# Products of state and C for two successive states in one GpSimd instruction, in a selective-scan recurrence

## The chip, the cores and the metric

The kernel runs on one core of one Trainium2 chip. The metric is the device time of one execution in microseconds, given as the median of several runs. A core has five engines with instruction queues of their own (TensorE for matmuls, VectorE, ScalarE, GpSimd, and SyncE, which here issues most DMAs). They meet through semaphores.

## The reference

Three layers follow each other on an input of shape (4, 64, 32, 32): a Mamba layer applied twice (to x and to x with its channels shuffled), causal attention, and a routed chain of feed-forward and attention steps. The change lies in the Mamba layer. Cut to its recurrence:

```
dt = softplus(x_dbl[..., :dt_rank] @ W_dt.T + b_dt)
A = -exp(A_log)
def step(h, inp):
    dt_t, B_t, C_t, u_t = inp
    dA = exp(dt_t[..., None] * A)
    h = dA * h + (dt_t * u_t)[..., None] * B_t[:, None, :]
    return h, einsum('bdn,bn->bd', h, C_t)
y = ys + u * D_skip
out = y * silu(z) @ W_out.T
```

There are 8 sequences (4 images, 2 kinds), each of length L = 1024, with 128 inner channels d and 16 states n. All is fp32.

## The kernel before, in words

The 128 inner channels lie on the partitions and the 1024 positions along the free dimension. The work is cut into 128 units: unit u is state n = u mod 16 of sequence q = u div 16. For each unit:

- the decay exp(dt * A_n), 128x1024, is made on ScalarE (L1155);
- the driving term dtu * B_n is made in one of two ways. For nine of the sixteen states TensorE broadcasts B_n into the PSUM bank pair pb (L690) and VectorE multiplies it by dtu (L1429). For the seven states in POOLED = (1, 4, 6, 8, 10, 12, 14) a DMA broadcasts B_n from DRAM into bb, and GpSimd multiplies (pool_drive, L1733, the tile dbu); ScalarE then writes the decay of that unit to pb;
- VectorE runs the scan h = decay * h + drive along the 1024 positions (L1434) into one of NHH = 4 buffers hh;
- GpSimd multiplies hh by C_n, which a DMA has broadcast into one of NCC = 4 buffers cc (pool_hc, L1722), into one of NHC = 3 buffers hc;
- TensorE adds hc to the PSUM accumulator py by matmuls with an identity (pe_sum, L702), LAG = 3 units behind.

After unit 15 VectorE multiplies py by the gate (dve_y, L1443, two halves), ahead of unit LAG of the next sequence. Between the units each engine does, at fixed states, pieces of the preparation of the next sequence: the input projection (pe_x, L633 and L634, at n = 0), the B and C rows (n = 3 to 6), and dt as a softplus (n = 7 to 12), with two VectorE steps called lost (L1405, after units 9 and 10) and two called dtu (L1415, after units 11 and 12). In sequences 2, 4 and 6 TensorE also does the output matmuls of a finished image (L721 at n = 13, L729 at n = 14). In sequence 7 the preparation of the attention takes the place of the next sequence: four VectorE steps (t1) after unit 6 and two (zq) after unit 12.

Every engine's order is written out by hand in loops over u. What ties them:

- GpSimd: the driving term of unit u + 2 comes ahead of the product of unit u; the product waits for the scan of u (scan_done), for C (c_in), and for the sum of unit u - NHC (hc_used);
- VectorE: the scan of unit u waits for its driving term, its decay, and the product of unit u - NHH (hc_done);
- TensorE, in iteration u: the B matmuls of unit u + 1 (they wait for the scan of u - 1), then the sum of unit u - LAG (it waits for hc_done), then the pieces of the next sequence;
- SyncE: C of unit u is requested when the product of u - NCC is done; B for pooled unit u + 3 follows it in the queue.

After the last unit TensorE's queue holds the first Q and K matmuls (pe_qk, L824 and L825), the early output matmuls (L721), and the last sums mixed with them.

Of the kernel before, what the change touches and what calls it, by code (L numbers as in the profile page):

```python
# [12 lines left out]
ALU = mybir.AluOpType  # L13
# [3 lines left out]
B, C, L = 4, 64, 1024  # L17
DI, NS, DR = 128, 16, 4
# [14 lines left out]
def atleast(eng, sem, value):  # L33

    if not isinstance(value, int) or value > 0:
        eng.wait_ge(sem, value)
# [332 lines left out]
def build_all(nc, w, inp, scr, out):  # L369

    ctx = ExitStack()
    with ctx:
        def sb(name, shape, dt=FP32):
            return ctx.enter_context(nc.sbuf_tensor(name, shape, dt))
# [6 lines left out]

        POOLED = (1, 4, 6, 8, 10, 12, 14)
        NP = len(POOLED)
        NHH, NHC, NCC, NDA, NDB, LAG = 4, 3, 4, 3, 2, 3
        LAST, UNITS, SKIP_AT, AHEAD = NSEQ - 1, NS * NSEQ, 8, 1

        u2_all = sb("u2_all", [DI, 2 * L])
# [11 lines left out]
        da = [sb(f"da_{i}", [DI, L]) for i in range(NDA)]  # L399
        hh_all = sb("hh_all", [DI, NHH * L])  # L400
        hh = [hh_all[:, i * L:(i + 1) * L] for i in range(NHH)]
        hc = [sb(f"hc_{i}", [DI, L]) for i in range(NHC)]
        cc = [sb(f"cc_{i}", [DI, L]) for i in range(NCC)]
        bb = [sb(f"bb_{i}", [DI, L]) for i in range(2 if NP else 0)]
        dbu = [sb(f"dbu_{i}", [DI, L]) for i in range(NDB if NP else 0)]
        ex, rl = sb("ex", [DI, L]), sb("rl", [DI, L])
# [5 lines left out]
        b_full, dbu_done, da_done, scan_done = sem("b_full"), sem("dbu_done"), sem("da_done"), sem("scan_done")  # L412
        pooled_done, hc_done, hc_used = sem("pooled_done"), sem("hc_done"), sem("hc_used")
# [22 lines left out]
        def pool_count(u):  # L436
            return NP * (u // NS) + sum(1 for n in POOLED if n < u % NS)

        def own_count(u):
            return u - pool_count(u)  # L440

        def outs_before(q):
            return max(0, (q - 1) // 2)
# [249 lines left out]
        def pe_sum(pe, u):  # L693
            if u < 0:
                return
            q, n = divmod(u, NS)
            pe.wait_ge(hc_done, u + 1)
            for r in range(2):
                if n == 0:
                    atleast(pe, y_free, 2 * (q - 1) + r + 1)  # L700
                for t in range(2):
                    last = nc.tensor.matmul(py[part(t), half(r)], ident[part(r), part(r)], hc[u % NHC][part(r), half(t)],  # L702
                                            start=(n == 0), stop=(n == NS - 1), skip_group_check=True)
                last.then_inc(hc_used, 1)
# [115 lines left out]
        def pe_qk(pe, c):  # L820
            pe.wait_ge(zq_done, c + 1)
            if c < 2:
                pe.wait_ge(scan_done, UNITS - 1 + c)
            nc.tensor.matmul(qk[c][0], w["wq1"][:, :], zq[:, col(c)], start=True, stop=True).then_inc(at.q_full, 1)  # L824
            nc.tensor.matmul(qk[c][1], w["wk1"][:, :], zq[:, col(c)], start=True, stop=True).then_inc(at.k_full, 1)  # L825
# [120 lines left out]
        def _(pe):  # L946
# [35 lines left out]
            for u in range(UNITS):  # L982
# [26 lines left out]
                if q == LAST:  # L1009
                    pe_first_pair(pe, n)  # L1010
            pe_qk(pe, 0)
            pe_first_pair(pe, NS)
            pe_sum(pe, UNITS - 3)
            pe_qk(pe, 1)
# [404 lines left out]
        def dve_unit(dve, u):  # L1419
            q, n = divmod(u, NS)  # L1420
            if n == 0:
                dve.wait_ge(dtu_done, 2 * q + 2)
            if pooled(u):
                dve.wait_ge(pooled_done, pool_count(u) + 1)
                decay, drive = pb[u % 2], dbu[pool_count(u) % NDB]
            else:
                k = own_count(u)
                dve.wait_ge(b_full, k + 1)
                nc.vector.tensor_tensor(pb[u % 2][:, :], pb[u % 2][:, :], dtu[q % 2][:, :], ALU.mult).then_inc(dbu_done, 1)  # L1429
                dve.wait_ge(dbu_done, k + 1)  # L1430
                decay, drive = da[k % NDA], pb[u % 2]
            dve.wait_ge(da_done, u + 1)
            atleast(dve, hc_done, u - NHH + 1)
            nc.vector.tensor_tensor_scan(hh[u % NHH][:, :], decay[:, :], drive[:, :], 0.0,  # L1434
                                         ALU.mult, ALU.add).then_inc(scan_done, 1)

# [275 lines left out]
            run(dve, dve_attend, dve_feed, dve_select)  # L1712


        def pool_hc(pool, u):
            pool.wait_ge(scan_done, u + 1)
            pool.wait_ge(c_in[u % NCC], 16 * (u // NCC + 1))
            if u < 2:
                for v in ((2,), (1, 3))[u]:
                    pool.wait_ge(xs_in[v], 32)  # L1720
            atleast(pool, hc_used, 2 * (u - NHC + 1))
            nc.gpsimd.tensor_tensor(hc[u % NHC][:, :], hh[u % NHH][:, :], cc[u % NCC][:, :], ALU.mult).then_inc(hc_done, 1)  # L1722

        def pool_drive(pool, u):
            if u >= UNITS or not pooled(u):
# [47 lines left out]
        def _(pool):  # L1773
# [55 lines left out]
            affine(1, 1)  # L1829
            for u in range(2):  # L1830
                pool_drive(pool, u)
            for u in range(UNITS):
                pool_drive(pool, u + 2)
                pool_hc(pool, u)
            pool.wait_ge(hc_used, 2 * UNITS)
            for t in wa:
                nc.gpsimd.memset(t, 0.0).then_inc(zeroed, 1)
# [47 lines left out]
        def sp_c(sp, u):  # L1885
            q, n = divmod(u, NS)
            if n == 0:
                sp.wait_ge(scr_in, 16 * (q + 1))
            atleast(sp, hc_done, u - NCC + 1)
            sp.dma_start(cc[u % NCC][:, :], scr[q % 2, NS + n:NS + n + 1, :].broadcast_to((128, L))).then_inc(c_in[u % NCC], 16)  # L1890

        def sp_b(sp, u):
# [132 lines left out]
```

## Time and profile before

| | |
|---|---|
| median of 3 runs | 763.95 us (763.78 to 768.19) |
| span of the profiled execution | 766.2 us |
| from its start to the first unit | 46 us |
| recurrence, 46 to 476 us | 430 us: GpSimd busy 426.75, VectorE 403.52, TensorE 331.65, ScalarE 288.99 |
| the rest, 476 to 766 us | 290 us: TensorE busy 247.62, VectorE 146.05, GpSimd 26.16 |

The profile is of one execution, on the one core. No time other than its span is recorded for the profiled execution, so the 766.2 us stand beside the median of the runs and not beside a time of its own. Busy time is the sum of the durations of an engine's instructions, overlaps counted once. A row of the timeline gives the start and duration in us, the engine, the line, the tiles and shapes and a count of merged instructions; in brackets stands idle time before it and what ended it. Successive instructions of one engine overlap slightly in their recorded durations, so the step from start to start is the better measure where there are several in a row.

### The profile page before, as it was taken

What the parts mean: (1) busy time and instruction counts of PE and PEld (TensorE: products, weight loads), DVE (VectorE), ACT (ScalarE), POOL (GpSimd) and SP (SyncE); (2) the same over time, 40 slices, a digit from 0 to 9 for tenths busy, and PEclk for the clock granted to TensorE, in tenths of its full rate; (3) what the DMA queues carried; (4) which work ended last, traced back from release to release, by engine and by line L of the source; (5) the groups of instructions that cost most, each with busy time, mean ns of one, the idle gap of its engine ahead of it and who ended that gap; (6) DMA issues with size and microseconds to landing.
All of it is one profiled execution on the core that took longest, in us unless ns stands there. A gap on an engine that the chain in (4) does not pass through costs nothing.

```text
span 766.2 us, 10774 instructions
## 1 busy us (share of the span) xinstructions
PE 607.6 (79%) x3563; PEld 257.1 (34%) x3591; DVE 570.3 (74%) x587; ACT 440.7 (58%) x662; POOL 474.0 (62%) x252
## 2 busy tenths in 40 slices
PE   3876686777986777967868879978976969999993
PEld 2321121121221212311212223446663335777741
DVE  3488998998998999999989997445562525666643
ACT  1887767587578677676775752544444224555520
POOL 6369999999999999999999998500002200000002
PEclk9999798898998998997989999989999889999997
DMA  3389677576665676666765761000000000000002
GB/s 96 83 266 297 220 240 234 199 260 232 215 237 216 223 255 216 241 229 204 261 231 201 255 228 58 1 1 2 2 12 3 6 15 1 2 1 2 1 2 60
DMA packets 33187, 105.47 MB, mean 138 GB/s; under 512 B 6997, under 2 KB 7518, under 8 KB 33118
## 3 DMA queue, kind: packets, MB, share of 16 engines
q1 hardware_dynamic: 32022, 103.94, 40.1%
q8 instruction: 34, 0.56, 0.3%
q10 hardware_dynamic: 776, 0.55, 0.3%
q0 software_dynamic: 320, 0.13, 0.1%
q14 instruction: 35, 0.29, 0.1%
HBM read 98.84 MB, written 2.10 MB: 132 GB/s over the span
## 4 chain that ended last, share of the span: by engine, by line
issue 34%; PE 24%; POOL 16%; DVE 15%; ACT 7%; DMA 2%; POOLq 0%; SPq 0%; DVEq 0%; ACTq 0%
POOL dbu L1733 7%; POOL hc L1722 7%; DVE hh_all L1434 7%; PE py L702 6%; DVE pb L1429 3%; PE py L229 2%; PE pb L198 2%; PE pb L690 2%; PE px L252 1%; PE px L729 1%; DMA cc<-scr 1%; POOL yg L1736 1%; DVE yg L1443 1%; ACT pb L1155 1%; DVE dtu_all L1415 1%
## 5 line engine op out<-in xcount | busy, mean ns | idle before, releaser
L1722 POOL TENSOR_TENSOR hc<-hh_all,cc 128x1024 f32<-128x1024 f32 x128 | 299.2, 2367 | 2.8 <-DMA cc<-scr 1.5
L702 PE MATMUL py<-hc,w_cst 64*64 64x512 f32 x1024 | 157.0, 673 | 26.3 <-POOL hc L1722 17.9
L1736 POOL TENSOR_TENSOR yg<-w_xs 128x512 f32<-128x512 f32 x12 | 15.2, 1266 | 247.2 <-DVE w_xs L1560 154.6
L1434 DVE TENSOR_TENSOR_SCAN hh_all<-da,pb 128x1024 f32<-128x1024 f32 x72 | 164.6, 2287 | 2.5
L1434 DVE TENSOR_TENSOR_SCAN hh_all<-pb,dbu 128x1024 f32<-128x1024 f32 x56 | 127.7, 2281 | 17.8 <-POOL dbu L1733 14.4
L1733 POOL TENSOR_TENSOR dbu<-bb,dtu_all 128x1024 f32<-128x1024 f32 x56 | 132.6, 2369 | 0.0
L690 PE MATMUL pb<-bc,w_sel 128*128 128x512 bf16 x118 | 42.2, 424 | 71.3 <-DVE hh_all L1434 67.3
L1155 ACT ACTIVATE pb<-dt_all,w_aneg 128x1024 f32<-128x1024 f32 x56 | 62.6, 1118 | 59.9 <-DVE hh_all L1434 58.2
L1429 DVE TENSOR_TENSOR pb<-pb,dtu_all 128x1024 f32<-128x1024 f32 x72 | 87.5, 1215 | 1.8 <-DVE dtu_all L1415 0.2
L285 DVE TENSOR_REDUCE gate_all<-pb 128x1 f32<-128x1024 f32 (+7 forms) x64 | 60.4, 986 | 32.8 <-PE pb L208 16.8
L1155 ACT ACTIVATE da<-dt_all,w_aneg 128x1024 f32<-128x1024 f32 x72 | 80.5, 1137 | 0.5
L702 PEld LDWEIGHTS py<-hc,w_cst 64*64 64x64 f32 x1024 | 31.0, 140 | 105.1 <-issue 56.9
L198 PE MATMUL pb<-dt_all,u_all 64*128 64x512 f32 (+3 forms) x208 | 51.4, 609 | 2.3 <-DVE w_xs L1506 1.2
L690 PEld LDWEIGHTS pb<-bc,w_sel 128*128 128x128 bf16 x144 | 9.5, 100 | 126.5 <-DVE hh_all L1434 101.7
L229 PE MATMUL py<-w_cst,dbu 128*128 128x128 f32 x208 | 29.4, 281 | 9.2 <-ACT dbu L328 5.3
L328 ACT ACTIVATE bb<-pb,gate_all 128x1024 f32<-128x1024 f32 (+4 forms) x32 | 28.6, 904 | 12.5 <-DVE gate_all L285 12.5
L336 ACT ACTIVATE da<-py 128x512 f32<-128x512 f32 (+2 forms) x28 | 13.7, 533 | 35.8 <-PE py L229 35.7
L336 ACT ACTIVATE cc<-py 128x512 f32<-128x512 f32 (+1 forms) x28 | 14.6, 564 | 33.3 <-PE py L229 33.3
L328 ACT ACTIVATE dbu<-pb,gate_all 128x1024 f32<-128x1024 f32 (+3 forms) x32 | 30.3, 957 | 4.7 <-DVE gate_all L285 4.7
L292 DVE COPY da<-py 128x512 f32<-128x512 f32 (+2 forms) x28 | 16.1, 610 | 20.6 <-PE py L229 20.6
L229 PE MATMUL py<-w_cst,bb 128*128 128x128 f32 x192 | 28.2, 287 | 3.9 <-ACT bb L328 3.9
L292 DVE COPY cc<-py 128x512 f32<-128x512 f32 (+1 forms) x28 | 17.2, 648 | 17.3 <-PE py L229 17.3
(290 smaller groups left out, 952.6 us busy)
## 6 DMA issues: line engine op xcount, KB each, us to landing
cc<-scr SPq DMA_DIRECT2D x128, 512.0 KB, 4.4
bb<-scr SPq DMA_DIRECT2D x56, 512.0 KB, 4.8
w_xs<-hc SPq DMA_DIRECT2D x6, 256.0 KB, 4.6
w_xst<-in_x SPq DMA_DIRECT2D x2, 512.0 KB, 5.3
scr<-bcf SPq DMA_DIRECT2D x8, 128.0 KB, 3.6
w_xs<-dt_all SPq DMA_DIRECT2D x4, 256.0 KB, 6.0
w_xs<-dtu_all SPq DMA_DIRECT2D x4, 256.0 KB, 5.6
out<-yg SPq DMA_DIRECT2D x8, 128.0 KB, 2.7
```

The costliest lines, as they stand in the source:

```text
L198: last = nc.tensor.matmul(self.s[r][:, o + a:o + a + m], self.qt[rows, g * 128:(g + 1) * 128], self.kt[rows, p * L + a:p * L + a + m], sta ...
L229: last = nc.tensor.transpose(self.pt[:, o + j:o + j + 128], self.p[g % 2][r][:, j:j + 128], self.w["cst"][:, IDN:IDN + 128])
L285: self.nc.vector.tensor_reduce(self.nm[:, i:i + 1], self.s[r][:, self.start(g):self.start(g) + 128 * self.blocks(g)], AX.X, ALU.max, negat ...
L292: self.nc.vector.tensor_copy(self.pts[g % 2][0][:, a:a + m], self.pt[:, a:a + m]).then_inc(self.pts_dve, 1)
L328: self.nc.scalar.activation(self.p[g % 2][r][:, 0:n], self.s[r][:, self.start(g):self.start(g) + n], ACT.Exp, bias=self.nm[:, i:i + 1], ac ...
L690: last = nc.tensor.matmul(pb[u % 2][:, half(h)], w["sel"][:, n, :], bc3[q % 2][:, half(h)], start=True, stop=True)
L702: last = nc.tensor.matmul(py[part(t), half(r)], ident[part(r), part(r)], hc[u % NHC][part(r), half(t)], start=(n == 0), stop=(n == NS - 1) ...
L1155: nc.scalar.activation(to[:, :], dt[q % 2][:, :], ACT.Exp, scale=w["aneg"][:, n:n + 1]).then_inc(da_done, 1)
L1429: nc.vector.tensor_tensor(pb[u % 2][:, :], pb[u % 2][:, :], dtu[q % 2][:, :], ALU.mult).then_inc(dbu_done, 1)
L1434: nc.vector.tensor_tensor_scan(hh[u % NHH][:, :], decay[:, :], drive[:, :], 0.0, ALU.mult, ALU.add).then_inc(scan_done, 1)
L1722: nc.gpsimd.tensor_tensor(hc[u % NHC][:, :], hh[u % NHH][:, :], cc[u % NCC][:, :], ALU.mult).then_inc(hc_done, 1)
L1733: nc.gpsimd.tensor_tensor(dbu[k % NDB][:, :], bb[k % 2][:, :], dtu[q % 2][:, :], ALU.mult).then_inc(pooled_done, 1)
```

## The change

The products of two successive units u and u + 1, u even, are made by one GpSimd instruction of 128x2048. The buffers of hc and cc become slices of one tensor each, as those of hh already are, and hc gets a fourth buffer. The first two and the last two units keep single products. hc_done now counts instructions, and hc_count(u) gives the count at which unit u's product is done. On GpSimd both driving terms (units u + 2 and u + 3, where they are pooled) stand ahead of the pair; with the states in POOLED, this moves one of the seven, that of state 1, ahead of the product of state 14. TensorE's sums lag by 4 units, y moves to unit 4, and one more sum stands behind the first Q and K matmuls at the end.

```diff
-        NHH, NHC, NCC, NDA, NDB, LAG = 4, 3, 4, 3, 2, 3
+        NHH, NHC, NCC, NDA, NDB, LAG = 4, 4, 4, 3, 2, 4
...
-        hc = [sb(f"hc_{i}", [DI, L]) for i in range(NHC)]
-        cc = [sb(f"cc_{i}", [DI, L]) for i in range(NCC)]
+        hc_all, cc_all = sb("hc_all", [DI, NHC * L]), sb("cc_all", [DI, NCC * L])
+        hc = [hc_all[:, i * L:(i + 1) * L] for i in range(NHC)]
+        cc = [cc_all[:, i * L:(i + 1) * L] for i in range(NCC)]
...
+        def hc_count(u):
+
+            if u < 2:
+                return u + 1
+            return 2 + u // 2 if u < UNITS - 2 else u + 3 - UNITS // 2
...
         def pe_sum(pe, u):
...
-            pe.wait_ge(hc_done, u + 1)
+            pe.wait_ge(hc_done, hc_count(u))
...
             pe_qk(pe, 0)
+            pe_sum(pe, UNITS - 4)
             pe_first_pair(pe, NS)
             pe_sum(pe, UNITS - 3)
...
         def dve_unit(dve, u):
...
-            atleast(dve, hc_done, u - NHH + 1)
+            atleast(dve, hc_done, hc_count(u - NHH))
...
-        def pool_hc(pool, u):
-            pool.wait_ge(scan_done, u + 1)
-            pool.wait_ge(c_in[u % NCC], 16 * (u // NCC + 1))
+        def pool_hc(pool, u, count):
+
+            pool.wait_ge(scan_done, u + count)
+            for v in range(u, u + count):
+                pool.wait_ge(c_in[v % NCC], 16 * (v // NCC + 1))
...
-            atleast(pool, hc_used, 2 * (u - NHC + 1))
-            nc.gpsimd.tensor_tensor(hc[u % NHC][:, :], hh[u % NHH][:, :], cc[u % NCC][:, :], ALU.mult).then_inc(hc_done, 1)
+            atleast(pool, hc_used, 2 * (u + count - NHC))
+            here = slice(u % NHC * L, (u % NHC + count) * L)
+            nc.gpsimd.tensor_tensor(hc_all[:, here], hh_all[:, here], cc_all[:, here], ALU.mult).then_inc(hc_done, 1)
...
-            for u in range(UNITS):
-                pool_drive(pool, u + 2)
-                pool_hc(pool, u)
+            for u in range(0, UNITS, 2):
+                if u in (0, UNITS - 2):
+                    for v in (u, u + 1):
+                        pool_drive(pool, v + 2)
+                        pool_hc(pool, v, 1)
+                else:
+                    for v in (u, u + 1):
+                        pool_drive(pool, v + 2)
+                    pool_hc(pool, u, 2)
...
         def sp_c(sp, u):
...
-            atleast(sp, hc_done, u - NCC + 1)
+            atleast(sp, hc_done, hc_count(u - NCC))
```

## Rows read from the trace of the kernel before

**Rows 1.** The page: span, and GpSimd's busy tenths in forty slices.

```profile
span 766.2 us, 10774 instructions
...
POOL 6369999999999999999999998500002200000002
```

**Rows 2.** The page's groups: shapes, count, busy, mean ns, idle before and its releaser.

```profile
L1722 POOL TENSOR_TENSOR hc<-hh_all,cc 128x1024 f32<-128x1024 f32 x128 | 299.2, 2367 | 2.8 <-DMA cc<-scr 1.5
...
L1736 POOL TENSOR_TENSOR yg<-w_xs 128x512 f32<-128x512 f32 x12 | 15.2, 1266 | 247.2 <-DVE w_xs L1560 154.6
...
L1434 DVE TENSOR_TENSOR_SCAN hh_all<-pb,dbu 128x1024 f32<-128x1024 f32 x56 | 127.7, 2281 | 17.8 <-POOL dbu L1733 14.4
L1733 POOL TENSOR_TENSOR dbu<-bb,dtu_all 128x1024 f32<-128x1024 f32 x56 | 132.6, 2369 | 0.0
...
L1429 DVE TENSOR_TENSOR pb<-pb,dtu_all 128x1024 f32<-128x1024 f32 x72 | 87.5, 1215 | 1.8 <-DVE dtu_all L1415 0.2
```

**Rows 3.** Timeline of GpSimd: products and sums in a row.

```profile
466.31 9.28 POOL L1722 TENSOR_TENSOR hc<-hh_all,cc 128x1024 f32<-128x1024 f32 x4
...
582.86 2.50 POOL L1736 TENSOR_TENSOR yg<-w_xs 128x512 f32<-128x512 f32 x2 [88.61 <-DVE w_xs L1540]
```

**Rows 4.** Timeline of GpSimd and VectorE, sequence 5, units 8 to 14.

```profile
345.97 4.65 POOL L1722 TENSOR_TENSOR hc<-hh_all,cc 128x1024 f32<-128x1024 f32 x2
...
359.84 6.97 POOL L1722 TENSOR_TENSOR hc<-hh_all,cc 128x1024 f32<-128x1024 f32 x3
...
346.04 2.29 DVE L1434 TENSOR_TENSOR_SCAN hh_all<-pb,dbu 128x1024 f32<-128x1024 f32 x1 [0.62 <-POOL dbu L1733]
...
359.93 2.27 DVE L1434 TENSOR_TENSOR_SCAN hh_all<-pb,dbu 128x1024 f32<-128x1024 f32 x1
```

**Rows 5.** Timeline of GpSimd and VectorE, first units of sequence 0.

```profile
50.62 4.67 POOL L1722 TENSOR_TENSOR hc<-hh_all,cc 128x1024 f32<-128x1024 f32 x2 [1.34 <-DVE hh_all L1434]
...
57.56 4.66 POOL L1722 TENSOR_TENSOR hc<-hh_all,cc 128x1024 f32<-128x1024 f32 x2
...
66.02 2.35 POOL L1722 TENSOR_TENSOR hc<-hh_all,cc 128x1024 f32<-128x1024 f32 x1 [1.50 <-DMA cc<-scr]
...
50.46 2.26 DVE L1434 TENSOR_TENSOR_SCAN hh_all<-pb,dbu 128x1024 f32<-128x1024 f32 x1
...
59.53 2.26 DVE L1434 TENSOR_TENSOR_SCAN hh_all<-pb,dbu 128x1024 f32<-128x1024 f32 x1
```

**Rows 6.** Timeline of VectorE and TensorE, ends of sequences 4 and 5.

```profile
306.72 2.29 DVE L1434 TENSOR_TENSOR_SCAN hh_all<-pb,dbu 128x1024 f32<-128x1024 f32 x1
...
371.38 1.21 DVE L1429 TENSOR_TENSOR pb<-pb,dtu_all 128x1024 f32<-128x1024 f32 x1
...
308.31 3.61 PE L729 MATMUL px<-yg,w_wts 64*64 64x512 f32 x16
...
318.33 1.09 PE L702 MATMUL py<-hc,w_cst 64*64 64x512 f32 x8
```

**Rows 7.** Timeline of VectorE, sequence 7: unit 7, then 8 and 12.

```profile
443.57 1.22 DVE L1429 TENSOR_TENSOR pb<-pb,dtu_all 128x1024 f32<-128x1024 f32 x1
444.83 2.29 DVE L1434 TENSOR_TENSOR_SCAN hh_all<-da,pb 128x1024 f32<-128x1024 f32 x1
447.03 2.27 DVE L1434 TENSOR_TENSOR_SCAN hh_all<-pb,dbu 128x1024 f32<-128x1024 f32 x1
...
459.78 2.26 DVE L1434 TENSOR_TENSOR_SCAN hh_all<-pb,dbu 128x1024 f32<-128x1024 f32 x1
```

**Rows 8.** Timeline of TensorE, end of sequence 7.

```profile
468.70 1.09 PE L702 MATMUL py<-hc,w_cst 64*64 64x512 f32 x8 [0.34 <-POOL hc L1722]
469.72 1.12 PE L824 MATMUL pb<-w_xs,w_wq 128*128 128x512 f32 x2
...
477.93 1.09 PE L702 MATMUL py<-hc,w_cst 64*64 64x512 f32 x8
```

**Rows 9.** Tile cc, 100 to 400 us: C's broadcasts from issue to landing.

```profile
DMA to landing us min/median/max: 3.4/4.3/5.4
```

## The prediction

> **What bounds the kernel now.** I read the page first: busy time per engine in forty slices [rows 1], then the groups by line [rows 2], then the timeline of GpSimd and VectorE over the recurrence. The slices show GpSimd at 9 tenths from the fourth slice to the twenty-fourth. The groups say what fills it: 128 products of 2367 ns and 56 driving terms of 2369 ns, with only 2.8 us of idle time before the products and none before the driving terms. From start to start one such instruction takes less than its duration: four products in a row occupy 9.28 us, so that the step is (9.28 - 2.35) / 3 = 2.31 us [rows 2, 3]. 184 x 2.31 = 425 us is the recurrence. A sequence (16 products, 7 driving terms) takes 23 x 2.31 = 53.2 us.
>
> VectorE is not far behind. From start to start its multiply takes 1.26 us and its scan 2.20 us [rows 7]. A sequence is 9 units with both, 7 with a scan alone, and six half-width steps (lost, dtu, y) that I put at 4 us together from the half of a 1215 ns multiply [rows 2]: 9 x 3.46 + 7 x 2.20 + 4 = 50.5 us. The 14.4 us that it waited for driving terms [rows 2] are those few per cent. So GpSimd sets the pace by about 5%, and any saving on it over 2.7 us per sequence would be cut by VectorE. The question is whether even a smaller saving gets through.
>
> **The saving.** 62 pairs of products become 62 instructions of 128x2048. The trace has no two-input instruction of that size. It has 128x512 and 128x1024: two of 512 in a row occupy 2.50 us at 1266 ns each, a step of 1.24 us [rows 2, 3]. From 1.24 and 2.31 us, each element costs 2.09 ns and each instruction 0.17 us beside its elements, so that a pair takes 2.31 + 2 x 1.07 = 4.46 us instead of 4.63. The bounds are 4.63 (nothing is saved) and 4.3 (twice the fixed part). I take 4.46, since both neighbours are measured and the form is the same. On GpSimd alone that is 62 x 0.17 = 10.3 us.
>
> The Trainium skill (GPSIMD Engine Reference, section Performance versus the Vector engine) gives 4497 ns for a two-input add of 2048 elements per partition. By that figure, as an estimate, the saving would be 0.13 us per pair and the whole sum about 1 us worse.
>
> **What the pairing demands.** Before, the product of unit u started when scan u was done. Now a pair u, u+1 starts only when scan u+1 is done, while the driving term that releases the scan of unit u+2 still stands one instruction ahead, and the scan of u+4 waits for the whole pair. So VectorE must be one unit further on at every even product, and it can't be: it is released by GpSimd itself at units 8 and 10. That handover shows as "0.62 <-POOL dbu" [rows 4]. I follow one sequence from the end of the driving term of unit 10.
>
> Stretch one, to the pair 12, 13. Before: two products, a driving term, two products, a driving term, 6 x 2.31 = 13.87 us, and that is what the rows show, 345.97 to 359.84. Scan 13 was done at 359.93, when scan 14 began [rows 4]. VectorE's chain from the driving term (scans 10 to 13, two multiplies, a "lost" and two "dtu" steps) is thus 13.96 us, in the other sequences 14.0 to 14.2. GpSimd would be ready after 2 x 4.46 + 2 x 2.31 = 13.54 us. The product follows a scan's end by 0.16 us (scan 1 starts at 50.46, which is the end of scan 0, and the first product at 50.62 [rows 5]). So the pair starts at 14.12: it waits 0.58 us.
>
> Stretch two, to the pair 0, 1 of the next sequence: pair, driving term of the next unit 1 (now ahead of the pair 14, 15), pair: 11.23 us. From the 359.93 + 0.16 of the same sequence, GpSimd would be ready at 371.32. Scan 1 was done at 371.38, when the multiply of unit 2 began [rows 6]; with 0.16 us that is a wait of 0.2. But this pair also needs the buffers of units 12 and 13, so the sum of unit 13 on TensorE, which with the lag of four comes behind the B matmuls of unit 2. In sequences without an output that sum ends about where scan 1 does, give or take 0.3. In sequences 2 and 4 TensorE is late: the output matmuls, two sums and the next input projection fill it from 308.31 without a gap, and the sum in that place starts at 318.33 [rows 6], ending near 319.3. GpSimd would be ready at 306.72 + 0.16 + 11.23 = 318.11. The pair starts at 319.43: a wait of 1.3 us, twice.
>
> Stretch three, pairs 0 to 6, four times 6.77 us. VectorE's two scans and the multiply between them are 5.66 us, and 1.18 us more where y (now ahead of unit 4) or a "lost" step falls: about 0.1 to 0.2 us late in all.
>
> A plain sequence is then 14.12 + 11.23 + 0.3 + 27.08 + 0.15 = 52.9 us against 53.2: 0.3 gained of the 1.3 saved. Sequences 2 and 4 are 14.12 + 11.23 + 1.3 + 27.08 = 53.75: 0.5 lost each. From sequence 0 to sequence 6, that is 4 x (-0.3) + 2 x 0.5 = -0.2 us.
>
> **Both ends.** In sequence 0 GpSimd is ahead of VectorE. The pair 2, 3 could start at 57.56, but scan 3 ends at 59.53, where scan 4 starts [rows 5]. The pair starts at 59.69, 2.1 us late. Then a wait for C that is in the rows anyway (1.50 us before 66.02) takes most of it: about 0.6 late after the pair 4, 5 and 0.3 by unit 10.
>
> In sequence 7 VectorE has more to do (four steps of t1 at unit 6, two of zq at unit 12) and runs almost without a gap. Scan 7 of it starts at 444.83 and ends at 447.03 [rows 7], so the pair 6, 7 starts at 447.2, 1.8 us after GpSimd would be ready for it (the pair 4, 5 starts at 438.6). GpSimd then ends the driving term of unit 12 at 447.2 + 2 x 6.77 = 460.7, where VectorE was ready for scan 12 at 459.78: VectorE loses 0.9 us, ends scan 13 at 467.6, and the pair 12, 13 (before: from 466.31) runs from 467.7 to 472.2. TensorE's last chain began with the sum of unit 12 at 468.70 and ran without a gap, by way of the first Q and K matmuls at 469.72, to the last sum at 477.93, 9.23 us [rows 8]. Now Q and K (about 1.9 us, two like the row of Q) go ahead of that sum, and the sum waits for the pair until 472.35; 9.23 - 1.9 = 7.3 us later, at 479.7, comes the last one, 1.7 us late.
>
> What follows is untouched. The memory cover: C for a pair is requested when the pair before the last is done, at least 6.77 us ahead, and landed in 3.4 to 5.4 us [rows 9]; two requests now start together, which I cost at nothing, and at up to 1 us per sequence where it fails. Waits on the y bank and on the bf16 pieces keep their distance, as one y step moves by one unit and its sum with it. Queue order on SyncE is unchanged.
>
> Sum: +0.3 (sequence 0), -0.2 (middle), +1.7 (end) = +1.8, all of it a difference. The profiled execution has a span of 766.2 us and lies 2.2 above the median of the runs; so I put it on the median: 763.95 + 1.8 = 765.7 us. Seen from GpSimd, the 10.3 us saved are spent as 7 x 0.6 before the pair 12, 13, about 4 at the seams, and the rest in the first and last sequence.
>
> **Rivals.** (1) The saving gets through. It needs VectorE to be ahead by a unit; for it speaks that its total is 2.7 us under GpSimd's per sequence, against it the waits of [rows 4]. If only the output seams and half of the other waits occur, some 6 us remain: 758; with a fixed part of 0.3 us, 754. Chance 0.15. (2) A pair of 4.63 us. Then stretch one waits 0.25, output seams 1.0, nothing is gained, and the ends cost the same or 1 us more: 7 x 0.3 + 2 x 1.0 + 3 = +7: 771. It decides from a pair over 4.6 us. Chance 0.10. (3) C is late. Three 512 KB transfers in a burst instead of one by one; the cover is 6.77 us less two SyncE issues, the longest landing 5.4 [rows 9]. From a landing of 6.2 us on, each sequence waits at the pairs 0, 1 and 2, 3: at 1 us each, +7 to +9, so 773. Slower. Chance 0.08. (4) The instruction is not run as one, or VectorE is held up by the longer GpSimd instruction: no row shows a scan lengthened beside a busy GpSimd (2281 ns in the mean of 56 [rows 2]). Chance 0.02, around 775. The forecast, waits eat the saving, 761 to 769, has 0.65.
>
> **Chances.** One per cent, 7.6 us, is about what a measurement of this kernel can tell from no change. Faster by more (under 756.3) takes half of rival 1: 0.08. Slower by more (over 771.6) takes rival 3, 4 and a part of rival 2: 0.12. Within: 0.80. The range from 758 to 771 leaves about 2 in 10 out.
>
> **What would show it.** In the new profile: products of 128x2048 at 4.5 us, 62 of them. GpSimd's busy time near 464 us, with some 11 us of new idle before the products, released by VectorE's scans and, in sequences 2 and 4, by TensorE's sums. VectorE's wait for driving terms smaller, not larger. The last sum near 479.7 us. The prediction is wrong if pairs start without waiting, or if pairs take well under 4.4 us, or if the idle before the products is put down to DMA.

## The result, and the profile after

The changed kernel takes 770.7 us (median of 4 runs, 768.3 to 773.0) beside 764.2 us for the kernel before (4 runs): a ratio of 1.0079, with an interval of 1.0053 to 1.0105. Measured a second time (e1, 6 runs beside 27 of the kernel before) it is 1.0061 [1.0040, 1.0082]. The forecast was 765.7 us, 0.7% less; the time is 0.3 us inside the upper end of the range (758 to 771).

The profiled executions hide this: their spans are 766.2 us before and 766.4 us after. They have to be read by stretches. I cut both at the same instructions: GpSimd's first product, the first memset of the code table behind the recurrence, and the first `yg` of the later stages. The first row is of the kernel before, the second of the one after (start, duration, engine, operation, idle time before it).

```profile
483.61 0.63 POOL L1755 MEMSET w_wts<- 1x646 f32 x1 [3.68 <-PE px L729]
```

```profile
486.76 0.63 POOL L1766 MEMSET w_wts<- 1x646 f32 x1 [3.69 <-PE px L736]
```

From the first product (50.62 and 50.87) to this row are 433.0 us before and 435.9 after: the recurrence has become 2.9 us longer. In e1, and in a new run of the kernel before (e5), the same two stretches are 436.9 and 432.7 us: 4.2 longer. What follows is the same list of instructions in both. The windows of TensorE over the first attention step, the feed-forward step and the second attention step (from:to, length, busy time and count, granted clock, DMA share, GB/s), before and then after:

```profile
483.61:582.86 99.25, 86.84 (x717) 0.95 0.02 3
582.86:603.33 20.47, 13.42 (x52) 0.83 0.02 4
603.33:745.85 142.52, 131.97 (x1085) 0.96 0.02 4
```

```profile
486.76:584.81 98.05, 85.59 (x717) 0.97 0.01 3
584.81:605.02 20.21, 13.46 (x52) 0.83 0.01 4
605.02:746.01 140.99, 130.48 (x1085) 0.98 0.02 4
```

The same 1085 matmuls took 142.5 us at a granted clock of 0.96 and 141.0 us at 0.98. That is 3.0 us over the three stretches, it went against the kernel before in this one execution, and it covers the loss. In the other executions below the second attention step is either 140.4 to 141.0 us or 142.5 to 142.9, whatever the kernel (e5, the kernel before again: 140.7). So I compare the stretch of the recurrence alone ("recurrence" below: first product to that memset), and the medians for the whole.

The groups of the page after that answer to [rows 2], and below them, from the answer that keeps shapes apart, the pairs alone:

```profile
L1442 DVE TENSOR_TENSOR_SCAN hh_all<-pb,dbu 128x1024 f32<-128x1024 f32 x56 | 127.8, 2282 | 19.7 <-POOL dbu L1744 16.0
L1744 POOL TENSOR_TENSOR dbu<-bb,dtu_all 128x1024 f32<-128x1024 f32 x56 | 132.1, 2359 | 0.0
...
L1437 DVE TENSOR_TENSOR pb<-pb,dtu_all 128x1024 f32<-128x1024 f32 x72 | 87.3, 1213 | 1.8 <-DVE dtu_all L1423 0.2
```

```profile
L1733 POOL TENSOR_TENSOR hc_all<-hh_all,cc_all 128x2048 f32<-128x2048 f32 x62 | 280.9, 4531 | 12.1 <-DVE hh_all L1442 6.8 <-PE py L709 4.9 <-issue 0.2
```

GpSimd now has 12.1 us of idle time before the pairs and 1.4 before its four single products (the page gives 13.4 for both), where the products had 2.8: 10.6 us are new (some 11 were forecast). 6.8 us end with a scan of VectorE, 4.9 us with a sum of TensorE. The scans take what they took (2282 ns, 2281 before), and VectorE's wait for driving terms rose from 14.4 to 16.0 us. The pair itself, on GpSimd's timeline in sequence 5, units 10 to 14:

```profile
355.05 4.54 POOL L1733 TENSOR_TENSOR hc_all<-hh_all,cc_all 128x2048 f32<-128x2048 f32 x1 [0.61 <-PE py L709]
359.55 2.35 POOL L1744 TENSOR_TENSOR dbu<-bb,dtu_all 128x1024 f32<-128x1024 f32 x1
361.96 4.51 POOL L1733 TENSOR_TENSOR hc_all<-hh_all,cc_all 128x2048 f32<-128x2048 f32 x1
366.43 2.37 POOL L1744 TENSOR_TENSOR dbu<-bb,dtu_all 128x1024 f32<-128x1024 f32 x1
```

From start to start the pair takes 366.43 - 361.96 = 4.47 us, against 2 x 2.31 = 4.63: 0.155 us saved per pair, 9.6 us for 62. The page gives GpSimd 466.1 us of work.

### The profile page after: what moved, and what is told of

Its sections match the earlier page's. It is cut to its first block, busy times and chain, and to the rows that moved or that the text cites. A ratio compares the mean times of both kernels' runs of the same rounds, so it can differ in the third digit from the quotient of the medians.

```text
span 766.4 us, 10739 instructions
## 1 busy us (share of the span) xinstructions
PE 615.0 (80%) x3591; PEld 260.5 (34%) x3591; DVE 570.2 (74%) x587; ACT 440.0 (57%) x662; POOL 466.1 (61%) x190
## 4 chain that ended last, share of the span: by engine, by line
issue 34%; PE 24%; DVE 19%; POOL 14%; ACT 5%; DMA 1%; POOLq 0%; SPq 0%; DVEq 0%; ACTq 0%
DVE hh_all L1442 9%; POOL hc_all L1733 8%; PE py L709 5%; DVE pb L1437 5%; POOL dbu L1744 4%; PE py L229 2%; PE pb L198 2%; PE px L736 2%; PE px L252 1%; POOL yg L1747 1%; PE pb L697 1%; DVE dtu_all L1423 1%; PE px L674 1%; PE px L675 1%; DMA cc_all<-scr 1%
## 5 line engine op out<-in xcount | busy, mean ns | idle before, releaser
L1733 POOL TENSOR_TENSOR hc_all<-hh_all,cc_all 128x2048 f32<-128x2048 f32 (+1 forms) x66 | 290.1, 4399 | 13.4 <-DVE hh_all L1442 8.1
L709 PE MATMUL py<-hc_all,w_cst 64*64 64x512 f32 x1024 | 154.6, 678 | 1.0 <-POOL hc_all L1733 0.6
L1442 DVE TENSOR_TENSOR_SCAN hh_all<-pb,dbu 128x1024 f32<-128x1024 f32 x56 | 127.8, 2282 | 19.7 <-POOL dbu L1744 16.0
L697 PE MATMUL pb<-bc,w_sel 128*128 128x512 bf16 x144 | 48.7, 423 | 85.8 <-DVE hh_all L1442 83.5
L709 PEld LDWEIGHTS py<-hc_all,w_cst 64*64 64x64 f32 x1024 | 33.3, 143 | 75.7 <-issue 65.1
L198 PE MATMUL pb<-dt_all,u_all 64*128 64x512 f32 (+3 forms) x208 | 49.4, 588 | 2.4 <-DVE w_xs L1514 1.2
L336 ACT ACTIVATE cc_all<-py 128x512 f32<-128x512 f32 (+1 forms) x28 | 14.5, 564 | 31.7 <-PE py L229 31.7
L292 DVE COPY cc_all<-py 128x512 f32<-128x512 f32 (+1 forms) x28 | 17.1, 648 | 17.3 <-PE py L229 17.3
```

The source lines that it names most:

```text
L198: last = nc.tensor.matmul(self.s[r][:, o + a:o + a + m], self.qt[rows, g * 128:(g + 1) * 128], self.kt[rows, p * L + a:p * L + a + m], sta ...
L292: self.nc.vector.tensor_copy(self.pts[g % 2][0][:, a:a + m], self.pt[:, a:a + m]).then_inc(self.pts_dve, 1)
L697: last = nc.tensor.matmul(pb[u % 2][:, half(h)], w["sel"][:, n, :], bc3[q % 2][:, half(h)], start=True, stop=True)
L1733: nc.gpsimd.tensor_tensor(hc_all[:, here], hh_all[:, here], cc_all[:, here], ALU.mult).then_inc(hc_done, 1)
```

## The experiments

"Idle" is GpSimd's idle time before pairs; where a kernel has single products too, theirs is not in it (in e7 the products of units 0, 1, 126 and 127). In e9, e10 and e12 a driving term more stands ahead of the first product, so that the recurrence is measured from a later point than in the other kernels; from the first scan of VectorE to the memset it is 435.4 us before, 435.2 in e9, 432.2 in e10 and 433.5 in e12. The kernel before is 764.4 us beside e1 to e4 (27 runs), 764.0 beside e5 to e8 and 764.7 and 764.9 beside e9 to e11 and e12.

| kernel | recurrence, us | idle, us | median, us | ratio to before, interval |
|---|---|---|---|---|
| before / e5, before again | 433.0 / 432.7 | - | 765.4 (e5) | 1.0009 [0.9993, 1.0026] |
| after / e1, after again | 435.9 / 436.9 | 12.1 / 12.9 | 769.1 (e1) | 1.0061 [1.0040, 1.0082] |
| e2 six product buffers | 433.6 | 9.6 | 767.9 | 1.0043 [1.0023, 1.0063] |
| e3 chosen pairs | 433.6 | 7.8 | 767.1 | 1.0031 [1.0014, 1.0047] |
| e4 chosen pairs, six buffers | 433.1 | 7.5 | 767.1 | 1.0036 [1.0017, 1.0054] |
| e6 no pairs | 432.6 | - | 765.4 | 1.0006 [0.9984, 1.0029] |
| e7 waits of pairs alone | 441.2 | 9.2 | 773.8 | 1.0132 [1.0106, 1.0159] |
| e8 pairs at units 4, 6, 8 | 433.6 | 5.2 | 767.5 | 1.0047 [1.0031, 1.0063] |
| e9 pairs, driving terms earlier | 431.9 | 11.0 | 762.7 | 0.9966 [0.9939, 0.9992] |
| e10 driving terms earlier, no pairs | 428.9 | - | 762.0 | 0.9964 [0.9942, 0.9986] |
| e11 pairs at 4, 6, 8, but not at the ends | 432.3 | 2.7 | 765.9 | 1.0023 [1.0003, 1.0043] |
| e12 driving terms earlier, 42 chosen pairs | 430.2 | 2.4 | 761.2 | 0.9948 [0.9930, 0.9965] |

**e1, the same kernel again**, to have a second profile of it beside the runs that follow.

> The changed kernel once more, with a profile from another execution. Theory W (the pairs' waits eat the saving): the recurrence ends 3 us later than before, whichever execution is profiled, and what the median shows beyond 3 us lies in the attention steps after it, where the two executions profiled so far already differ by 3 us; the median falls between 767 and 771. Rival T (the change costs something after the recurrence): the stretch from the end of the recurrence to the end is longer than before's by 3 us in every execution, median 770 to 772.

The recurrence was 436.9 us, the idle time 12.9 us. The three stretches behind it took 259.2 us, and 260.0 in e5: the change costs nothing there. Sequence 1 took 53.7 us here and 52.7 in the first profile, and this difference has a cause that can be read. In its units 7 to 10 stand the matmuls of the time step (L674, L675), which wait for ScalarE. TensorE's timeline there, after and then e1:

```profile
132.29 1.04 PE L697 MATMUL pb<-bc,w_sel 128*128 128x512 bf16 x2 [4.35 <-DVE hh_all L1442]
...
135.53 1.13 PE L674 MATMUL px<-ex,w_cst 128*128 128x512 f32 x2 [0.28 <-ACT px L1131]
136.49 1.02 PE L675 MATMUL px<-rl,w_cst 128*128 128x512 f32 x2
```

```profile
131.78 0.60 PE L697 MATMUL pb<-bc,w_sel 128*128 128x512 bf16 x2 [3.69 <-DVE hh_all L1442]
...
135.60 2.07 PE L674 MATMUL px<-ex,w_cst 128*128 128x512 f32 x2 [1.75 <-ACT px L1131]
137.47 1.91 PE L675 MATMUL px<-rl,w_cst 128*128 128x512 f32 x2
...
139.31 1.23 PE L709 MATMUL py<-hc_all,w_cst 64*64 64x512 f32 x8
...
140.78 4.54 POOL L1733 TENSOR_TENSOR hc_all<-hh_all,cc_all 128x2048 f32<-128x2048 f32 x1 [1.26 <-DVE dtu_all L1423]
```

The same four matmuls take 2.1 us in the one and 4.0 in the other: from 135 to 140 us the granted clock was 0.96 in the first profile and 0.53 in e1, which ran them at the lower of the clock's two levels (1.2 GHz in place of 2.4). The sum behind them ends at 139.31 + 1.23 = 140.54, and the next pair (last row, GpSimd) starts 0.24 us later, after a wait of 1.26 us that it did not have in the first profile. The row names a step of VectorE that ended at about the same time; the same 0.24 us lie between the end of the sum and the pair where the row names TensorE (354.81 and 355.05 in the first profile). Of seven such places the first profile has five in which L674 takes 1.8 to 2.1 us instead of 1.1, e1 all seven; the kernel before had five too (at 188.51, for instance) and no product there waited for TensorE.

**e2, six buffers for the products** (as in all kernels below that mix sizes, a slice is taken per tile by its own number of buffers).

```diff
-        NHH, NHC, NCC, NDA, NDB, LAG = 4, 4, 4, 3, 2, 4
+        NHH, NHC, NCC, NDA, NDB, LAG = 4, 6, 4, 3, 2, 4
```

> The changed kernel with six hc buffers instead of four, so that no pair waits for a sum on TensorE. Theory W: the 4.9 us of GpSimd idle time that TensorE ended (two of 1.4 us at the seams after sequences 2 and 4, and three smaller) go; 1 to 2 us come back as waits for scans; 3 us faster than the changed kernel. A rival (VectorE is the limit and TensorE's waits are hidden anyway): within 1 us of the changed kernel.

```profile
L1738 POOL TENSOR_TENSOR hc_all<-hh_all,cc_all 128x2048 f32<-128x2048 f32 x62 | 280.7, 4531 | 9.6 <-DVE hh_all L1447 9.3 <-DMA cc_all<-scr 0.2
```

Against the 4.9 us of the row after, nothing is left behind TensorE; part of it came back behind VectorE (9.3 against 6.8). The recurrence is 2.3 to 3.4 us shorter than with four buffers: the waits for TensorE's sums cost about 3 us, where I had charged 2 x 1.3. The median moved by only 1.2 us (769.1 to 767.9), and the intervals of the two ratios overlap.

**e3 and e4, pairs only where the plan saw room** (units 2, 4, 6, 8, 10 and 14, without unit 2 of the first and 6 and 14 of the last sequence; e4 with six buffers as well).

```diff
-                if u in (0, UNITS - 2):
+                if not paired(u):
...
+        def paired(u):
+            q, n = divmod(u, NS)
+            return n in (2, 4, 6, 8, 10, 14) and (q, n) not in ((0, 2), (LAST, 6), (LAST, 14))
```

> Pairs only where VectorE is ahead: states 2, 4, 6, 8, 10 and 14; single products at 0 and 12, at state 2 of sequence 0 and at states 6 and 14 of the last sequence: 45 pairs. Theory W: 45 x 0.155 = 7.0 us saved on GpSimd, two waits for TensorE of 1.1 and 0.6 us left: 5 us faster than before, 759. Rival T: the cost after the recurrence stays, 762 or more. A rival by which the saving never gets through (VectorE is the real limit): 764.

> Chosen pairs as in the run before it, with six hc buffers. Theory W: no waits left on GpSimd beside those of the kernel before, all of 7 us gained, 757. Rivals as in the run before it: 762, or 764.

This was my largest miss: 433.6 and 433.1 us, not a gain but the kernel before, and medians of 767.1 us that are 0.3 and 0.4% above it where 759 and 757 were expected. The waits had not gone, they had moved. The rows are e3's and then e4's pairs, and below them one wait of e4 that no plan of mine had:

```profile
L1738 POOL TENSOR_TENSOR hc_all<-hh_all,cc_all 128x2048 f32<-128x2048 f32 x45 | 203.8, 4529 | 7.8 <-PE py L714 4.2 <-DMA cc_all<-scr 2.3 <-DVE hh_all L1447 0.9
```

```profile
L1738 POOL TENSOR_TENSOR hc_all<-hh_all,cc_all 128x2048 f32<-128x2048 f32 x45 | 204.1, 4535 | 7.5 <-DVE hh_all L1447 5.5 <-DMA cc_all<-scr 2.1
...
218.52 4.54 POOL L1738 TENSOR_TENSOR hc_all<-hh_all,cc_all 128x2048 f32<-128x2048 f32 x1 [1.50 <-DVE hh_all L1447]
```

With six buffers GpSimd comes sooner to unit 2 of a sequence, and then waits there for VectorE instead. In e3 TensorE's sums held other pairs (1.25 us at the pair 10, 11 of sequence 1, 1.33 at the pair 8, 9 of the last), and C held the pair 4, 5 of the first sequence by 2.3 us. So the theory "each wait is a local mishap; leave it out and its saving stays" was wrong.

**e5 and e6, the kernel before again, and the new one with its lag of four, its order and its layout, but no pair** (`paired` returns False).

> The kernel before against itself: the bound of what the medians can tell, and a profile of another execution than the first. Expected: a ratio of 1.000 within 0.002; the recurrence ends at 483.6 us again within 0.5, as GpSimd has no gap in it, and the attention steps after it take 278 to 280 us where the first profile had 282.6.

> The changed kernel with no pairs at all: single products in the old order, but with a lag of four, four hc buffers, y at unit 4 and the new order of the last sums. Theory W (the waits of the pairs cost the time): 764.4, as before. Rival L (the lag and the order of the sums, or the layout in one tensor, cost it): 766.5 or more.

432.7 and 432.6 us, ratios 1.0009 and 1.0006. The later sums and the slices of one tile cost nothing that can be seen. The loss belongs to the pairs.

**e7, the waits of the pairs without their saving.** Each pair is two products of 128x1024 with the pair's waits ahead of both and its signal behind both.

```diff
-            nc.gpsimd.tensor_tensor(hc_all[:, here], hh_all[:, here], cc_all[:, here], ALU.mult).then_inc(hc_done, 1)
+            for v in range(u, u + count):
+                last = nc.gpsimd.tensor_tensor(hc[v % NHC][:, :], hh[v % NHH][:, :], cc[v % NCC][:, :], ALU.mult)
+            last.then_inc(hc_done, 1)
```

> The changed kernel with its waits, but each pair made by two instructions of 128x1024: the waits without the saving. Theory W: a pair takes 4.63 us instead of 4.475; outside the stretches that VectorE sets (about half of a sequence) that is added to the time: 4 to 5 us over the changed kernel, 773 to 774. Rival (the saving never reaches the time): as the changed kernel, 769.

441.2 us, and 773.8 in the median. The waits alone cost 441.2 - 432.9 = 8.3 us (432.9: mean of before and e5). With the saving of 9.6 us added (after, e1) the recurrence is 436.4 (mean of 435.9 and 436.9): the saving gives back 4.8 (4 to 5 were expected), half of itself. This is the clearest single run of the study, since nothing but the size of the instruction differs from the kernel after.

**e8, pairs at units 4, 6 and 8 only** (`n in (4, 6, 8)`).

> Pairs only at states 4, 6 and 8, the ones that GpSimd makes while VectorE waits for driving terms (24 pairs in all). Theory W, as refined by the chosen pairs (GpSimd sets the pace only between unit 4 and unit 10, VectorE in the rest of a sequence): 3 x 0.155 us per sequence, 3 us below the kernel without pairs. Rival L: the same 3 us below the kernel without pairs, but that one is slower than before.

Where GpSimd sets the pace at all shows on VectorE's timeline. These are rows of e11, which has the same pairs, from scan 12 of sequence 3 on:

```profile
245.08 2.29 DVE L1447 TENSOR_TENSOR_SCAN hh_all<-pb,dbu 128x1024 f32<-128x1024 f32 x1 [0.24 <-DVE dtu_all L1428]
247.29 0.67 DVE L1428 TENSOR_TENSOR dtu_all<-px,u_all 128x512 f32<-128x512 f32 x1
...
260.67 2.29 DVE L1447 TENSOR_TENSOR_SCAN hh_all<-pb,dbu 128x1024 f32<-128x1024 f32 x1
...
269.77 1.26 DVE L1456 TENSOR_TENSOR yg<-py,gate_all 128x512 f32<-128x512 f32 x2
270.95 2.28 DVE L1447 TENSOR_TENSOR_SCAN hh_all<-pb,dbu 128x1024 f32<-128x1024 f32 x1
...
276.86 2.29 DVE L1447 TENSOR_TENSOR_SCAN hh_all<-pb,dbu 128x1024 f32<-128x1024 f32 x1 [0.19 <-POOL dbu L1749]
...
283.65 2.29 DVE L1447 TENSOR_TENSOR_SCAN hh_all<-pb,dbu 128x1024 f32<-128x1024 f32 x1 [1.05 <-POOL dbu L1749]
...
290.45 2.29 DVE L1447 TENSOR_TENSOR_SCAN hh_all<-pb,dbu 128x1024 f32<-128x1024 f32 x1 [0.48 <-POOL dbu L1749]
```

These are the scans 12, 1, 4, 6, 8 and 10. From 245.08 to 276.67 no row has an idle time; only at units 6, 8 and 10 does VectorE wait for GpSimd. In the kernel before it is the same (idle times of 0.21, 1.20 and 0.61 us at these units of sequence 6, none from 353.44 to 385.17). So I take it that a saving on GpSimd can shorten the sequence at those units alone. e8 pairs only there, and from one y to the next the sequences took 52.7 to 53.2 us against 52.8 to 53.6 before. But its total, 433.6 us, was not the 3 us shorter that I expected, and its median is 0.5% above the kernel before. Two waits are new: 2.68 us for C at unit 4 of the first sequence, and 1.71 us for VectorE at unit 6 of the last. GpSimd of e8:

```profile
62.12 2.34 POOL L1749 TENSOR_TENSOR dbu<-bb,dtu_all 128x1024 f32<-128x1024 f32 x1
67.15 4.53 POOL L1738 TENSOR_TENSOR hc_all<-hh_all,cc_all 128x2048 f32<-128x2048 f32 x1 [2.68 <-DMA cc_all<-scr]
```

**e11, e8 without these two pairs** (`(q, n) not in ((0, 4), (LAST, 6))`).

> Pairs only at states 4, 6 and 8 and without those of unit 4 of sequence 0 (a wait for C) and unit 6 of the last (a wait for the t1 steps): 22 pairs. Theory W: none of them waits, 22 x 0.155 = 3.4 us is saved on GpSimd, some 2 to 3 of it reaches the end of the recurrence (430 us instead of 432.8), median 762. Rival V: nothing, 765.

432.3 us: 0.6 below the kernel before in the profile, where 430 was expected, and 765.9 us in the median, where 762 was; the ratio of 1.0023 [1.0003, 1.0043] is if anything a loss. The 22 pairs save 3.4 us of GpSimd's work, and no gain can be measured. A wait of 1.34 us for a sum of TensorE now stands before the pair 8, 9 of the last sequence.

**e9 and e10, driving terms two units earlier.** The chain that the prediction followed starts with a driving term that VectorE waits for. With a third buffer for driving terms and for B they stand two units further ahead: the handover is no longer tight, at the same work. e9 has all pairs, e10 none.

```diff
-        NHH, NHC, NCC, NDA, NDB, LAG = 4, 4, 4, 3, 2, 4
+        NHH, NHC, NCC, NDA, NDB, LAG = 4, 4, 4, 3, 3, 4
...
-            for u in range(2):
+            for u in range(4):
...
-                        pool_drive(pool, v + 2)
+                        pool_drive(pool, v + 4)
...
-                sp_b(sp, u + 3)
+                sp_b(sp, u + 5)
```

> The changed kernel with the driving terms two units earlier on GpSimd (that of unit u + 4 ahead of the product of u) and three buffers each for B and the driving terms, so that VectorE isn't held at units 8 and 10 and can be a pair ahead. Theory W: the waits before the pair 12, 13 and at the seams go or shrink under 0.3 us, a plain sequence takes 52.0 to 52.3 us against 53.2, the recurrence is 5 to 7 us shorter than before and the median 758 to 759. Rival V (VectorE's own 50.9 us and its waits set the pace anyway, the pairs only show it): no sequence under 52.8 us, recurrence as in the chosen pairs, 764 to 766.

> The control to the run before it: driving terms two units earlier, three buffers each, and single products. Theory W: GpSimd had no gap in a sequence before, so a lead alone gives nothing: 764 to 765, the recurrence 432.7 us. Rival V': VectorE gains by the lead itself, and the recurrence is shorter by over 1 us without any pair.

e9: 0.9966, and a median of 762.7 us where 758 to 759 was expected. The sequences without an output fell to between 52.2 and 52.5 us (53.2 to 53.6 before): here a saving gets through. Those with an output took 53.4, the pair 14, 15 waiting up to 1 us for TensorE's sums, against 52.8 and 52.9 before, and the ends cost what they did (C again by 2.43 us in the first sequence). Two waits of e9:

```profile
258.61 4.53 POOL L1733 TENSOR_TENSOR hc_all<-hh_all,cc_all 128x2048 f32<-128x2048 f32 x1 [1.03 <-PE py L709]
...
446.02 4.51 POOL L1733 TENSOR_TENSOR hc_all<-hh_all,cc_all 128x2048 f32<-128x2048 f32 x1 [1.59 <-DVE hh_all L1442]
```

e10, without any pair, reached the same: 0.9964. Its memset row stands at 480.93, against 483.61 before. I had expected nothing of it in the middle and got nothing: GpSimd worked without a gap but for 1.3 us. The 2.7 us are at the ends: from its product 8 of one sequence to that of the next GpSimd took 53.2 us in all six, as in the kernel before. The driving term of unit 4 fills GpSimd's first idle time (the 1.34 us of [rows 5]), and at the end GpSimd's last product is done 1.4 us nearer to TensorE's last sum, 2.12 us instead of 3.56 ahead of its release (first row e10, second the kernel before):

```profile
476.46 0.64 POOL L1859 MEMSET hc_all<- 128x128 f32 x4 [2.12 <-PE py L714]
```

```profile
479.14 0.64 POOL L1837 MEMSET hc<- 128x128 f32 x4 [3.56 <-PE py L702]
```

Together that is the 2.7 us. So the lead was worth having, and the pairs added nothing to it: in e9 the same six sequences are 3.1 us shorter than in e10, but its ends are longer by more, and its memset stands at 483.01. The profiled executions of e9 and e10 were the second longest of twelve each.

**e12, both, with 42 pairs in the six middle sequences, none at unit 14** (`0 < q < LAST and n % 2 == 0 and n != 14`).

> The driving terms two units earlier, as in the two runs with the lead, and pairs only in sequences 1 to 6, at all even states but 14 (the pair 14, 15 had waited 0.5 to 1.0 us for a sum on TensorE); single products in sequences 0 and 7 and at 14. 42 pairs, 6.5 us on GpSimd. Theory W: with VectorE ahead the saving gets through where neither engine waits: sequences of 52.0 to 52.5 us, the recurrence 424 to 426 us against 428.9 with the lead and no pairs, the median 758 to 759.5. Rival V (VectorE and TensorE set the sequences with the lead too): as the lead without pairs, 762.

761.2 us, 0.9948 [0.9930, 0.9965]: the lowest median of the study, 0.9 us under e10's, which their intervals do not tell apart. In the profile, of the longest of its eight executions, its memset is 0.7 us behind e10's. So the rival of this run, that the pairs add nothing to the lead (762 us), is not excluded. I had expected a recurrence of 424 to 426 us, and one sequence of 54.6 us took part of that away. Its pair 0, 1 of sequence 4 waits for a sum, and TensorE ahead of that sum runs the input projection at half speed, in the windows 250 to 256 and 256 to 261 at a granted clock of 0.54 and 0.53:

```profile
254.96 1.98 PE L714 MATMUL py<-hc_all,w_cst 64*64 64x512 f32 x8 [0.77 <-POOL hc_all L1738]
256.88 2.07 PE L645 MATMUL px<-w_xs,w_wts 128*128 128x512 f32 x2
258.74 1.92 PE L646 MATMUL px<-w_xs,w_wts 128*128 128x512 f32 x2
...
261.43 1.02 PE L646 MATMUL px<-w_xs,w_wts 128*128 128x512 f32 x2
...
264.13 4.54 POOL L1738 TENSOR_TENSOR hc_all<-hh_all,cc_all 128x2048 f32<-128x2048 f32 x1 [2.29 <-PE py L714]
```

## Why the prediction was near, and where it was wrong

The forecast was a loss of 1.8 us. The recurrence lost 2.9 and 4.2 us, the medians 6.6 and 4.6. The direction and the mechanism (waits that use up the saving) were right, and the size was too small. That 770.7 us still lies in the range is owed to the width of the range: it is 0.3 us from its end, and above the 761 to 769 us that I had given this mechanism.

**The saving** was right: 4.47 us a pair (4.46 forecast, 4.63 the bound), 466 us of work (464 forecast). Its total was a little high: 0.17 us for 62 pairs are 10.5 us, which I wrote as 10.3, and 9.6 were measured. The Trainium skill's figure for this size, 4497 ns (GPSIMD Engine Reference, section Performance versus the Vector engine), lies between the step of 4.47 us and the duration of 4531 ns that the trace shows, within 1% of both.

**Stretch one** was right: a wait of 0.58 us before the pair 12, 13 was forecast, and 0.48 to 0.50 is there in five of eight sequences, put down to VectorE's scan. In sequence 4 it stands beside the seam:

```profile
307.68 4.52 POOL L1733 TENSOR_TENSOR hc_all<-hh_all,cc_all 128x2048 f32<-128x2048 f32 x1 [0.50 <-DVE hh_all L1442]
...
320.45 4.53 POOL L1733 TENSOR_TENSOR hc_all<-hh_all,cc_all 128x2048 f32<-128x2048 f32 x1 [1.41 <-PE py L709]
```

**The output seam** was right as well: 1.3 us twice, and the rows have 1.40 and 1.41, in the places named. TensorE shows the reason given, the output matmuls and the next input projection ahead of the sum that releases the pair (319.13 + 1.09 = 320.22):

```profile
309.11 3.61 PE L736 MATMUL px<-yg,w_wts 64*64 64x512 f32 x16
...
319.13 1.09 PE L709 MATMUL py<-hc_all,w_cst 64*64 64x512 f32 x8
```

**Both ends** were right: 2.1 us late at the pair 2, 3 (2.10 measured) and 1.8 at the pair 6, 7 of the last sequence (1.81).

```profile
59.94 4.52 POOL L1733 TENSOR_TENSOR hc_all<-hh_all,cc_all 128x2048 f32<-128x2048 f32 x1 [2.10 <-DVE hh_all L1442]
...
448.64 4.52 POOL L1733 TENSOR_TENSOR hc_all<-hh_all,cc_all 128x2048 f32<-128x2048 f32 x1 [1.81 <-DVE hh_all L1442]
```

From that pair to TensorE's last sum I forecast 479.7 - 447.2 = 32.5 us, and it is 32.4. But the pair started 1.4 us later than forecast, so the last sum is at 481.08:

```profile
481.08 1.09 PE L709 MATMUL py<-hc_all,w_cst 64*64 64x512 f32 x8
```

**The step that failed is the price of TensorE's sums in the middle.** The middle was forecast at -0.2 us from sequence 0 to 6. Measured from y to y, the six sequences take 319.5 us before, 320.4 after and 321.5 in e1: +0.8 and +2.0. The ends, forecast at +2.0, came to 2.1 us after and 2.0 to 2.2 in e1, so the middle holds the error. From GpSimd's product 8 of one sequence to that of the next, where the kernel before takes 53.2 us each time, the four plain sequences took 52.7 to 53.0 us after (52.9 forecast) and 52.7 to 53.7 in e1. The two with an output took 54.6 and 54.1, and 54.0 and 54.6 in e1, where 53.75 was forecast (53.9, had I added the 0.15 us of stretch three as in the plain ones).

I charged the sums at the two output seams, 1.3 us each, and in plain sequences as falling "about where scan 1 does". Without that wait an output sequence is by my own stretches a plain one, 0.3 us gained, and six of them are -1.8 us: in the middle the sums were priced at 1.8 - 0.2 = 1.6 us. With six buffers (e2) the six sequences take 318.0 us, 1.5 less than before, so the part without TensorE held within 0.3 us, and the sums cost 2.4 us after and 3.5 in e1. The ones I missed stand before the pair 10, 11, 1.08 and 0.61 us after (the second is the row at 355.05): this pair needs the buffer of unit 7, whose sum stands behind the time-step matmuls, and both times TensorE ran them at its lower clock (0.52 granted from 349.5 to 354 us). TensorE before that pair, in the kernel after:

```profile
346.69 0.73 PE L697 MATMUL pb<-bc,w_sel 128*128 128x512 bf16 x2 [4.31 <-DVE hh_all L1442]
...
349.93 2.07 PE L674 MATMUL px<-ex,w_cst 128*128 128x512 f32 x2 [0.58 <-ACT px L1131]
351.79 1.91 PE L675 MATMUL px<-rl,w_cst 128*128 128x512 f32 x2
353.64 1.17 PE L709 MATMUL py<-hc_all,w_cst 64*64 64x512 f32 x8
```

The sum ends at 354.81 and the pair starts at 355.05. Before, a late sum in this place had nobody waiting for it; the pairs made the clock's fall cost something.

**The half that gets through** was in the forecast too. It priced the waits with a pair of 4.63 us at +7 us (rival 2) and with 4.46 us at +1.8, so that 5.2 of 10.3 us reach the time; e7 measured 8.3 us, and 4.8 of 9.6 us reach it. VectorE without idle time for 31.6 us of every 53 (rows of e11) is the reason that I see for it; the half fits it and does not prove it. That VectorE's wait for driving terms would fall was wrong: it rose from 14.4 to 16.0 us (14.6 in e1), and in e7 to 22.2.

**The rivals.** The first, that the saving gets through, is refuted by the waits themselves, and e7 gives it its half. The second falls with the pair's 4.47 us. The third, C late, did not decide the kernel after (no wait for a DMA before a pair in its first profile, one of 0.46 us in e1), though C's median from issue to landing rose from 4.4 to 4.8 us; it did show at the start in e3, e4, e8 and e9, with waits of 2.1 to 2.7 us.

**What stays open.** The recurrence accounts for 2.9 to 4.2 us of a median difference of 4.6 to 6.6. The profiled executions of e1 and e5 lie at their medians (769.2 beside 769.1, 765.8 beside 765.4), and between these two the recurrence's 4.2 us cover the whole difference of 3.4. The median of e5 is also 1.4 us above that of the other executions of the same kernel beside it, so that 1 to 2 us may be the spread of medians; the 6.6 us of the first measurement rest on four executions of each kernel. The rest may be in executions that no profile holds: the profiled one of the kernel after was the shortest of its four. The same holds for e3, e4 and e8, which lie 2.7 to 3.4 us above the kernel before in the median and only 0.2 to 0.7 in the recurrence of their one profile; the profiled ones were the fourth, third and second shortest of twelve. That was not shown.

Whether the pairs themselves make TensorE's clock fall more often was not tried either. L674 took 802 ns in the mean after and 893 in e1 (over the seven places), 818 before and 784 in e5, which does not tell. The granted clocks of all executions point that way: 0.925 in the mean in e1 beside 0.931 of the kernel before, 0.921 in e8 and 0.916 in e7 beside 0.929, with 0.928 in e5 and 0.927 in e6; but e9, with all pairs and the lead, had 0.930 beside 0.931. Which causes which, the waits or the falls, no run separates.

I also set the sum of 1.8 us straight onto the median, 2.2 us below the profiled span. The profiled execution of the kernel before, by its span the one of 768.2 us, was 4.2 us above that median, and its stretches behind the recurrence were 3.0 us longer than those of the kernel after, so the choice carries that much doubt.

## What to carry to other kernels

When two engines hand work to each other through rings of two to four buffers, merging two instructions of one of them saves its fixed part (0.155 us here) and demands that the other be a whole unit further on; count that first, at every place where that engine has no idle time, since there the saving turned into waiting. Look at each buffer that the merged instruction now needs two of, and at every sequence's order on the engine that frees it, not at the seams alone, and cost its work at the lower clock too: 4.9 us of the 12.1 us of idle time before the pairs came from there. A larger lead between the two engines (a third buffer for the driving terms, 0.9964 without any pair) was worth more than the merging, and its gain stood at the two ends of the recurrence.

## What the runs showed of the hardware

TensorE's clock reaches into a stretch that GpSimd and VectorE bound: two time-step matmuls took 2.07 us instead of 1.13 in five of seven sequences after and in all seven in e1, and the pair behind them waited up to 1.26 us. The kernel before had the same falls free of charge. The idle time just before the matmuls does not decide at which level they run. The first row is e1's, slow after 0.29 us of idle time, the second e11's, fast after 1.62:

```profile
82.34 2.08 PE L674 MATMUL px<-ex,w_cst 128*128 128x512 f32 x2 [0.29 <-ACT px L1131]
```

```profile
133.97 1.12 PE L679 MATMUL px<-ex,w_cst 128*128 128x512 f32 x2 [1.62 <-ACT px L1136]
```

The same 1085 matmuls of the second attention step ran in 140.4 to 141.0 us or in 142.5 to 142.9, in one and the same kernel too (before 142.5 at a granted clock of 0.96, before again 140.7 at 0.98). A single profile of this kernel, whose end is bound by TensorE, is therefore good to about 2 us in that stretch (3.0 us over the three), and two spans of 766 us proved nothing. I also had not expected that two C broadcasts requested at once would land only 0.4 us later in the median than one by one (4.8 against 4.4 us, 512 KB each).
